# A graph layer's aggregation: the widest of eight count tables is built and used first instead of last

## The reference

```python
xn  = _layernorm(x)
deg = segment_sum(1, dst)            # own node included
h   = xn @ W
out = segment_sum(h[src] * dinv[src] * dinv[dst], dst) + conv_bias
...
q, k, v = split(rmsnorm(xn, g_pre) @ w_qkv)      # attention: softmax of k over nodes, of q over 32 features
context = einsum('bhdn,bhen->bhde', k, v);  out = einsum('bhde,bhdn->bhen', context, q)
x = x + graph_part + attention_part;   x = x + experts(layernorm(x))
```

## Time and profile before

| What | Value |
|---|---|
| Device time, median of 3 runs | 1373.26 us (1373.19 to 1373.59) |
| Span of the profiled execution | 1377.2 us |
| PE, PEld, DVE, ACT, POOL busy | 1245.3, 1106.3, 962.4, 539.3, 854.3 us |
| Aggregation phase, first gather to last addition | 142.8 to 786.1 us |
| PE's granted clock in the 40 slices | mostly 0.9 or more, 0.7 to 0.8 in two slices of the phase and its end |

### The profile page before, as it was taken

The page is one execution under the profiler, slowest core; times in us unless marked ns, Lnnn a source line. Parts: engine busy times, 40 slices in busy tenths (PEclk is TensorE's granted clock), DMA queues, the critical chain, the costliest instruction groups (busy, mean ns, idle before and its releaser), DMA issues. The chain is left out here.

```text
span 1377.2 us, 30864 instructions
## 1 busy us (share of the span) xinstructions
PE 1245.3 (90%) x8354; PEld 1106.3 (80%) x8355; DVE 962.4 (70%) x2966; ACT 539.3 (39%) x1443; POOL 854.3 (62%) x836
## 2 busy tenths in 40 slices
PE   4997688999899999999898797985799999999998
PEld 4984687887788888887787686873699999999997
DVE  8998787887888777778693288998444444444444
ACT  7707301222333333333311101446455555555553
POOL 1294677777777777777777202431376666666665
PEclk9999899999999999999999898995799999999999
DMA  7005333335666666789898400449244444444443
GB/s 245 0 0 183 111 106 103 107 105 172 194 194 199 198 191 202 207 246 277 260 288 261 144 1 16 138 155 318 64 77 66 68 71 69 72 69 70 71 69 42
DMA packets 138148, 186.89 MB, mean 136 GB/s; under 512 B 21438, under 2 KB 116468, under 8 KB 137916
## 3 DMA queue, kind: packets, MB, share of 16 engines
q0 software_dynamic: 43440, 90.29, 28.7%
q1 hardware_dynamic: 94604, 95.40, 21.8%
HBM read 153.16 MB, written 33.41 MB: 135 GB/s over the span
## 5 line engine op out<-in xcount | busy, mean ns | idle before, releaser
L740 POOL DMA_INDIRECT RG<-table,srci x484 | 477.3, 986 | 153.0 <-issue 149.4
L757 PEld LDWEIGHTS ps<-S_t,RG 128*128 128x128 f32 x1936 | 259.2, 196 | 39.0 <-DMA RG<-table,srci 28.6
L757 PE MATMUL ps<-S_t,RG 128*128 128x96 f32 x1936 | 266.4, 278 | 21.6 <-DMA RG<-table,srci 21.1
L780 PE MATMUL ps<-zrow,R 128*128 128x256 f32 (+1 forms) x784 | 221.1, 389 | 15.2 <-DMA zrow<-table 8.7
L2010 POOL DMA_INDIRECT out<-R,S_t x105 | 166.3, 1584 | 99.5 <-DVE R L1980 55.8
L1893 PE MATMUL ps<-R,RG 128*128 128x128 f32 x1680 | 207.3, 277 | 0.0
L1893 PEld LDWEIGHTS ps<-R,RG 128*128 128x128 f32 x1680 | 198.3, 194 | 0.4 <-issue 0.4
L1903 PE MATMUL ps<-R 128*128 x840 | 198.5, 379 | 0.0
L1014 DVE TENSOR_TENSOR R<-R,ps 128x245 f32 (+4 forms) x300 | 142.1, 474 | 73.7 <-PE ps L768 52.5
L1926 ACT ACTIVATE R<-ps,RG 128x128 f32<-128x128 f32 x420 | 120.0, 368 | 175.8 <-PE ps L1893 175.8
L1976 DVE TENSOR_TENSOR R<-ps,R 128x256 f32<-128x256 f32 x105 | 44.6, 425 | 200.8 <-PE ps L1903 200.8
(11 more groups left out here) (360 smaller groups left out, 1989.9 us busy)
## 6 DMA issues: line engine op xcount, KB each, us to landing
zrow<-table SPq DMA_DIRECT2D x384, 128.0 KB
RG<-table,srci POOLq DMA_INDIRECT x484, 3.3
ntable<-R SPq DMA_DIRECT2D x12, 516.0 KB
table<-RG SPq DMA_DIRECT2D x12, 512.0 KB, 2.9
out<-R SPq DMA_DIRECT2D x12, 512.0 KB, 3.2
R<-in_x SPq DMA_DIRECT2D x6, 896.0 KB, 11.7
R<-in_w SPq DMA_DIRECT2D x8, 514.0 KB, 6.4
slot<-in_x SPq DMA_DIRECT2D x32, 128.0 KB
```

Source lines behind the costliest of these rows:

```text
L740: nc.gpsimd.indirect_dma_start(out=grows[:, s, :], out_offset=None, in_=table, in_offset=bass.IndirectOffsetOnAxis(ap=srci[:, ND + q, c:c ...
L757: last = nc.tensor.matmul(window(q % 2)[:, h, :], grows[:, s, h * P:(h + 1) * P], S_t[:, q % 2, c, :], start=c == 0, stop=c == GC - 1)
L780: nc.tensor.matmul(psD[:, 0:D], adj[b % 2][0:n, j, :], zrow[0:n, i % ZR, :], start=j == 0, stop=j == T - 1).then_inc(z_used, 1)
```

## The change

The eighth block's table is built and used first. `TURN` gives the order of the blocks by their place: 7, 0, 1, ..., 6. `SEQ` gives the chunks in that order and `FIRSTK` the place of each block's first chunk. The counts' semaphores now count places in `SEQ`, and the chunk's own column is looked up through it. `BUILT` and `USED` are redrawn: the first table has 20 chunks instead of 108 and is ready after step 6 instead of 32, so products run in steps 7 to 118 instead of 33 to 118. The side stages are moved and stretched: A over 14 steps instead of 12, C over 26 instead of 20, B over 45 instead of 51, D over 26 instead of 28.

```diff
-        A0, A1 = 0, 12
-        C0, C1 = 14, 34
-        B0, B1 = 37, 88
-        D0, D1 = 91, GQ - 2
-        BUILT = (0, 33, 47, 61, 74, 86, 95, 104, 112)
-        USED = (33, 47, 61, 74, 86, 95, 104, 112, GQ - 2)
+        A0, A1 = 0, 14
+        C0, C1 = 16, 42
+        B0, B1 = 45, 90
+        D0, D1 = 93, GQ - 2
+        TURN = (NDB - 1,) + tuple(range(NDB - 1))
+        BUILT = (0, 7, 36, 50, 63, 76, 88, 99, 109)
+        USED = (7, 36, 50, 63, 76, 88, 99, 109, GQ - 2)
+        SEQ = [m for b in TURN for m in range(DBLK[b][0] * GC, DBLK[b][1] * GC)]
+        FIRSTK = [SEQ.index(DBLK[b][0] * GC) for b in TURN] + [MD]
...
-            for (g0, g1), lo, hi in zip(DBLK, BUILT, BUILT[1:]):
-                for m in share(q, lo, hi, (g1 - g0) * GC):
-                    yield g0 * GC + m
+            for p, (lo, hi) in enumerate(zip(BUILT, BUILT[1:])):
+                for i in share(q, lo, hi, FIRSTK[p + 1] - FIRSTK[p]):
+                    yield FIRSTK[p] + i
...
-        def block_of(m):
-            return next(b for b, (g0, g1) in enumerate(DBLK) if m < g1 * GC)
+        def turn_of(i):
+            return next(p for p in range(NDB) if i < FIRSTK[p + 1])
+
+        def wide_of(i):
+            return DWB[TURN[turn_of(i)]]
...
-                        pe.wait_ge(cnt_ok, DBLK[b][1] * GC)
+                        pe.wait_ge(cnt_ok, FIRSTK[b + 1])
...
-                    at = nc.vector.value_load(first_i[0:1, DBLK[b][0]:DBLK[b][0] + 1], min_val=0, max_val=N - 1)
+                    at = nc.vector.value_load(first_i[0:1, DBLK[TURN[b]][0]:DBLK[TURN[b]][0] + 1], min_val=0, max_val=N - 1)
...
-                    nc.vector.tensor_scalar(hotk[m % 4][:, 0:wide], iokey[:, 0:wide], key[:, m:m + 1], None, ALU.is_equal)
+                    nc.vector.tensor_scalar(hotk[m % 4][:, 0:wide], iokey[:, 0:wide], key[:, SEQ[m]:SEQ[m] + 1], None, ALU.is_equal)
...
-                    b = block_of(m)
-                    at = nc.vector.value_load(off_i[0:1, m % GC, m // GC:m // GC + 1], min_val=0, max_val=DLIM)
+                    b, col = turn_of(m), SEQ[m]
+                    at = nc.vector.value_load(off_i[0:1, col % GC, col // GC:col // GC + 1], min_val=0, max_val=DLIM)
...
-                    if m == DBLK[b][0] * GC:
+                    if m == FIRSTK[b]:
```

More of the change, by code:

```diff
@@ L766, in count @@
                         pe.wait_ge(cnt_ok, m - 1)
-                    wide = T * DWB[block_of(m)]
+                    wide = T * wide_of(m)
                     nc.tensor.matmul(psK[m % 2][:, 0:wide], hots[m % 4], hotk[m % 4][:, 0:wide], start=True,
@@ L997, in chunk_onehots @@
                         v.wait_ge(cnt_ps, m - 3)
-                    wide = T * DWB[block_of(m)]
-                    nc.vector.tensor_scalar(hotk[m % 4][:, 0:wide], iokey[:, 0:wide], key[:, m:m + 1], None, ALU.is_equal)
-                    nc.vector.tensor_scalar(hots[m % 4], iokey[:, 0:P], slo[:, m:m + 1], None,
+                    wide = T * wide_of(m)
+                    nc.vector.tensor_scalar(hotk[m % 4][:, 0:wide], iokey[:, 0:wide], key[:, SEQ[m]:SEQ[m] + 1], None, ALU.is_equal)
+                    nc.vector.tensor_scalar(hots[m % 4], iokey[:, 0:P], slo[:, SEQ[m]:SEQ[m] + 1], None,
                                             ALU.is_equal).then_inc(key_ok, 1)
                 def chunk_add(m):
-                    b = block_of(m)
-                    at = nc.vector.value_load(off_i[0:1, m % GC, m // GC:m // GC + 1], min_val=0, max_val=DLIM)
+                    b, col = turn_of(m), SEQ[m]
+                    at = nc.vector.value_load(off_i[0:1, col % GC, col // GC:col // GC + 1], min_val=0, max_val=DLIM)
                     v.wait_ge(cnt_ps, m + 1)
@@ L1009, in chunk_add @@
                         v.wait_ge(cnt_ok, m)
-                    if m == DBLK[b][0] * GC:
+                    if m == FIRSTK[b]:
                         v.wait_ge(clear, b + 1 if b < 2 else 2 + (b - 1) * NWC)
-                    wide = DWB[b]
+                    wide = wide_of(m)
                     win = adj[b % 2][:, :, bass.ds(at, wide)]
```

## The result

| Kernel | Median of runs | Ratio to before, 95% interval |
|---|---|---|
| before | 1373.42 us (1373.19 to 1377.11, 4 runs) | |
| after | 1361.82 us (1358.75 to 1363.86, 4 runs) | 0.9899 [0.9878, 0.9919] |
| after, second series | 1365.11 us beside 1373.40 | 0.9938 [0.9919, 0.9956] |
| after, third series | 1364.04 us beside 1374.30 | 0.9924 [0.9903, 0.9944] |

The change makes the kernel faster, by 11.6, 8.3 and 10.3 us in three series. The forecast was 1363.9 us.

What follows compares the result with a forecast made beforehand. POOL's gathers set the pace while PE keeps up, with PE 19.2 us behind at the end. Last gather 4.3 us later, last addition 5.5 after it: 9.4 us less, span 1367.8, less 3.9 gives 1363.9 us; 8 in 10: 1358 to 1375.

Steps and rivals of the forecast that it cites:

- (1): Steps 0 to 6: building the 20 wide counts costs DVE more, taken as 1 us of PE backlog.
- (2): Steps 0 to 15: 49 products move to steps 7 to 35; 3.4 us hide in PE's gaps, backlog 10.5 at step 15.
- (3): Steps 16 to 35: PE needs 101.7 us against POOL's 100.2, backlog +1.5.
- (4): Steps 36 to 89: PE needs 289.2 us, 25.5 of it surcharge, against POOL's 270.5; backlog +18.7.
- (5): Mostly steps 40 to 89: backlog would come to 23.7 us against a 19.4 limit, so POOL is held up 4.3.
- rival A: Middle steps: PE absorbs the new products in handshake gaps, nothing is held up; 13.7 us less, 1359.6 us; 22%.
- (6): Steps 90 to 118: fewer products, lighter DMA load; PE wins back over 20 us of backlog and needs 14.
- (7): Phase end: the last addition comes 5.5 us after the last gather.
- POOL's own delays: Gathers slowed beside DVE instructions with two SBUF inputs: of POOL's 18 us, kept unchanged, give or take 3.
- B: Early work costs all that the end wins, 0.13 us more over 74 steps: 1373.3 us, no change; 15%.
- C: Steps 7 to 35: the counts' handshake with DVE makes them 171 us, POOL held up 27: 1387 us; 14%.
- D: Last 28 steps: PE waits for gathers and its clock falls, seven steps at 1.2 GHz: 1373 us; 5%.

Runs made afterwards that it cites:

- side stages only: The kernel before with only the side stages A, B, C and D at after's steps, tables in old order and steps: 1375.84 us, 1.0018 of before.
- same order, tables: The kernel before, table order kept, table steps redrawn: first built in 30 steps, last used over steps 109 to 118: 1367.54 us, 0.9955 of before.
- same order, all redrawn: The kernel before, table order kept, table steps redrawn (first built in 30 steps) and after's side stages added: 1365.26 us, 0.9923 of before.
- PSUM edit, flatter: After with the residual's second inputs in PSUM, queries in steps 45 to 93, residual from 97, table steps redrawn: 1366.09 us, 0.9924 of before.
- one-hots by tensor_scalar: After with each group's one-hots made by four tensor_scalars of 96 columns instead of one tensor_tensor: 1363.72 us, 0.9919 of before.
- both edits: After with one-hots made by four tensor_scalars and the residual's second inputs in PSUM: 1364.11 us, 0.9913 of before.
- order only: After with the side stages at before's steps, so only the tables' order and steps are new: 1376.82 us, 1.0021 of before.
- the later pair: After with the residual's second inputs in PSUM, measured again beside after: 1356.87 us, 0.9873 of before, 7.2 us less than after.

## Why the prediction was right

The step that carries it, backlog at the end turned into nothing but the last group's own chain, is shown by after's rows and by the experiments that undo one part each. By the steps:

- (1), (2) Backlog at step 15: 10.5 expected, 233.60 - 222.68 = 10.9.
- (3) Steps 16 to 35: 101.7 expected, 336.45 - 233.60 = 102.9.
- (4) **The mis-sized term.** Steps 36 to 89: 289.2 us expected, 613.26 - 336.45 = 276.8 measured. Of that 263.7 is the priced work, so the surcharge was 13.1 us, not 25.5. I had read the surcharge of before as a cost of each step. Much of it was slack: at a backlog of about 10 us PE still met moments in which its next rows weren't there. In before, from group 49's addition to group 89's:

```profile
PE ps L757 <- DMA RG<-table,srci: 7.7, 17, 0.8
```

  I had put 4.5 us down to such waits for all 52 steps. In after the same steps show none. This is what the stretch gives in eight kernels (start to start of the additions, against the prices of the work in it):

| Kernel | Priced | Observed | Over, per step | PE's waits for gathers | POOL's waits for PE, whole phase |
|---|---|---|---|---|---|
| before | 189.3 | 203.8 | 0.36 | 7.7 | 3.6 |
| after | 195.6 | 200.7 | 0.13 | 0 | 3.0 |
| side stages only | 197.2 | 202.6 | 0.13 | 0 | 3.0 |
| same order, tables | 195.4 | 199.3 | 0.10 | 0 | 11.0 |
| same order, all redrawn | 203.3 | 206.8 | 0.09 | 0 | 6.6 |
| PSUM edit, flatter | 184.9 | 198.9 | 0.35 | 6.4 | 3.7 |
| one-hots by tensor_scalar | 195.6 | 209.2 | 0.34 | 0 | 15.9 |
| both edits | 195.6 | 209.5 | 0.35 | 0 | 12.5 |

  From before to after, more priced work took less time: 6.3 us more to do, 3.1 us less to do it in. Where PE waits for gathers the time over the prices is partly slack; in the last two rows it is a real cost, DVE's. It is real in "order only" too: steps 16 to 35 there took 0.50 us each over their prices with no wait for a gather.
- (5) The peak of the backlog came out as said (454.85 - 435.44 = 19.4 us at group 57), but POOL was not held up by 4.3 us. Its 3.0 us of waits for PE are ten of 0.30 us each, and 0.30 is the gap that stands before every gather; only in group 120 of before was a gap longer (0.83). With 12.4 us less in (4), nothing was left of the 4.3. The limit of 19.4 us was also put too low, since PE's backlog reached 22.8 us with the order only. So rival A (22%), by which nothing is held up, is what happened here, though not for its reason: in steps 50 to 89 of before PE's waits in the handshake between counts and DVE were 0.2 us, and those for gathers 7.7.
- (6) Backlog at group 90 was 13.8 us and at 110 it was 7.0; the DMA share fell from 0.88 to 0.84. Both as said.
- (7) The end took 6.7 us, not 5.5. The last 32 matmuls in after, which answer to the earlier trace rows, and the last wait for a gather before them:

```profile
760.17 0.46 PE L763 MATMUL ps<-S_t,RG 128*128 128x96 f32 x2 [2.13 <-DMA RG<-table,srci]
...
763.93 0.69 PE L793 MATMUL ps<-ident,R 128*128 128x128 f32 x2 [0.81 <-ACT R L934]
764.41 5.56 PE L763 MATMUL ps<-S_t,RG 128*128 128x96 f32 x32
```

  They took 5.56 us where 4 x 0.87 = 3.5 would do: the first 19 start some 0.21 us apart, the others 0.11, so the first ran at the lower level again (granted clock 0.65 from 762 to 771 us). In the second and third profiles of after the end took 7.8 and 5.9 us.
- POOL's own delays were kept as the traces had them: 763.77 - 142.8 less 483 x 1.252 leaves 16.2 us, against 19.3 before. The comparison with the Trainium skill (SBUF — State Buffer, Who interferes with whom) came out for the row: the section has it, as an inference, that tensor_tensor with two SBUF inputs doesn't hold descriptor generation up, yet the delays shrank when just such instructions were given an input in PSUM (18.9 to 12.4 us in the later pair) or replaced by tensor_scalars (to 7.5). The same section also says that an instruction with two SBUF inputs contends with a GpSimd instruction that reads SBUF; the gathers read their indices, `srci`, from SBUF, and that sentence fits what was measured.
- Two readings of the schedule before were off, with little effect: steps 0 to 6 had 22 counts, not 23, and besides the 3 products of step 33 there were 7 in steps 34 and 35.

The forecast of the time is closer than its terms, and that is in part luck. The phase ended 6.2 us sooner than my sum (770.46 against 776.65): POOL's hold-up of 4.3 us didn't come, its own delays were 3.1 us less, and the end took 1.2 us more. The profiled span is 7.0 us under the forecast one (1360.8 against 1367.8). But the median is only 2.1 us under the forecast, because I took 3.9 us off the span for before's long execution, and after's median lies 1.0 above its span: 4.9 us of the error cancel there. (Other profiled executions have a span 1.8 us under their time, so the profile of before, 1377.2, belongs to an execution longer than all four of the first series, which end at 1377.11.) Rival A's 1359.6 is as near to the measured 1361.82 as the forecast; the time can't decide between them, the rows of (5) do.

The other rivals: B (no gain) is excluded by the intervals. C put steps 7 to 35 at 171 us; they took 336.45 - 184.51 = 151.9, that is 5.24 a step, and PE waited 2.6 us for L1020 in them (8.1 in the whole phase). D did not happen; the granted clock from 591 to 763 us was 0.99 (0.97 and 0.98 in the other profiles of after). The Trainium skill's HAM oscillation (TensorE: Matmul & The Clock Gate), by which matmuls lose their clock over and over to waits for DMA, is thus hardly seen here: PE waits for gathers again (23.8 us for the whole phase against 21.1), and the clock stayed. The lower level at the end of the phase came behind two waits for gathers, of 1.20 and 2.13 us.

## What to carry to other kernels

Where two engines run side by side and one falls behind only at the end, look at how the work is spread before asking for faster instructions: moving it to where the slower one has slack gave 8 to 12 us with not one operation less. Time over the priced work of a stretch is partly slack as long as the engine still waits for its inputs there, so look for those waits before carrying it over to a fuller stretch. And a stretch that is filled past its limit gives it all back (1.0021 where the side stages were left as they were), so the lists that share an engine have to be redrawn together. When an edit makes one engine faster and the time stays, compare the pace of the others before blaming the meeting of the two: the edit may have slowed them.

## What the runs showed of the hardware

A gather that starts while DVE runs an instruction with both inputs in SBUF takes longer: 0.17 us on average for the 63 under L977 in the second profile of after, 0.26 us for the 22 under L1080 in the first, up to 2.1 us in all. With one input in PSUM, or as a tensor_scalar of 96 columns, that is gone or nearly: the 18 gathers that start under the residual's scaled multiplication with its input in PSUM last 0.002 us longer, the 14 under its addition 0.03, and the 86 under the new tensor_scalars 0.017 us. I had kept these delays as given; taking a third of them away (the residual's) was worth 7.2 us, nearly as much as the change itself. Taking the one-hots' share away with four instructions in place of one cost DVE 0.26 us a step (0.48 to 0.74), and the gain was lost.
